# Mixture-of-experts layer of a vision block: down products with the weights stationary, summed in PSUM over all experts, gates applied to the activations

## What is computed

```
up_s   = einsum('th,seh->tse', xt, shared_up)                 # 2 shared experts
shared = einsum('tse,she->th', gelu(up_s), shared_down)
probs  = softmax(xt @ router_w.T)                             # 16 routed experts
gate   = top-4 of probs per token, elsewhere 0
act    = gelu(einsum('th,reh->tre', xt, routed_up)) * gate[:, :, None]
routed = einsum('tre,rhe->th', act, routed_down)
h      = h + shared + routed
```

## Time and profile before

| | us |
|---|---|
| three runs | 155.59, 155.68, 156.61 (median 155.68) |
| the profiled execution, whole | 155.6 |
| its span, first to last instruction | 153.8 |
| TensorE busy in the span | 148.0 (96%) |
| VectorE, ScalarE, GpSimd busy | 114.1, 102.2, 60.3 |
| granted TensorE clock | 1.00 |

### The profile page before, as it was taken

The page is one execution under the profiler, slowest core; times in us unless marked ns, Lnnn a source line. Parts: engine busy times, 40 slices in busy tenths (PEclk is TensorE's granted clock), DMA queues, the critical chain, the costliest instruction groups (busy, mean ns, idle before and its releaser), DMA issues.

```text
span 153.8 us, 3280 instructions
## 1 busy us (share of the span) xinstructions
PE 148.0 (96%) x1089; PEld 138.7 (90%) x1089; DVE 114.1 (74%) x370; ACT 102.2 (66%) x290; POOL 60.3 (39%) x50
## 2 busy tenths in 40 slices
PE   6989999999999999999999999999999999999992
PEld 2878799998897898999889999999999999999991
DVE  0058768768897776586765758997989679959982
ACT  0306999786689999999586398847583744636700
POOL 0004999456736544403119400332517323354000
PEclk9999999999999999999999999999999999999999
DMA  4999910000000499600000000000000000000004
GB/s 146 341 382 365 402 35 0 0 0 9 0 0 0 142 428 419 242 2 6 0 0 4 0 0 0 0 6 0 2 0 4 0 2 0 0 4 0 4 2 158
DMA packets 5892, 11.95 MB, mean 78 GB/s; under 512 B 931, under 2 KB 3699, under 8 KB 5747
## 3 DMA queue, kind: packets, MB, share of 16 engines
q1 hardware_dynamic: 4434, 9.79, 17.2%
q10 hardware_dynamic: 1440, 1.95, 3.6%
HBM read 11.13 MB, written 0.61 MB: 76 GB/s over the span
## 4 chain that ended last, share of the span: by engine, by line
PE 77%; ACT 8%; DVE 6%; DMA 3%; ACTq 2%; issue 1%; POOL 1%; DVEq 0%
PE bank L1047 61%; PE bank L1164 5%; PE bank L1071 5%; DMA aux_sb<-aux_w 3%; ACT probs L505 3%; PE bank L1136 2%; PE bank L1188 1%; ACT swapped L494 1%; ACT swapped L493 1%; PE bank L1152 1%; PE bank L1091 1%; DVE qk L726 1%; ACTq L241 1%; ACTq L244 1%; POOL swapped L399 1%
## 5 line engine op out<-in xcount | busy, mean ns | idle before, releaser
L414 POOL TENSOR_TENSOR exp_lo<-ffn_sb,exp_hi 128x512 fp32r<-128x512 f32 x18 | 23.5, 1314 | 40.5 <-ACT exp_hi L527 40.5
L839 DVE SCALAR_TENSOR_TENSOR h<-bank,gate,h 128x256 f32<-128x256 f32 (+1 forms) x80 | 32.3, 473 | 1.1 <-PE bank L1047 0.9
L1047 PE MATMUL bank<-exp_hi,act_hi 128*128 128x256 f32 (+1 forms) x90 | 25.5, 284 | 0.1
L1047 PE MATMUL bank<-exp_lo,act_hi 128*128 128x256 f32 (+1 forms) x90 | 25.2, 280 | 0.0
L1047 PE MATMUL bank<-exp_hi,act_lo 128*128 128x256 f32 (+1 forms) x90 | 25.2, 280 | 0.0
L819 DVE TENSOR_TENSOR act_lo<-act,act_hi 128x256 fp32r<-128x256 f32 (+1 forms) x36 | 17.9, 522 | 5.8 <-ACT act_hi L539 5.6
L1047 PE MATMUL bank<-hnT_hi,exp_hi 128*128 128x256 f32 (+1 forms) x72 | 21.8, 303 | 0.0
L536 ACT ACTIVATE act<-bank 128x256 f32<-128x256 f32 (+1 forms) x36 | 15.3, 424 | 9.6 <-PE bank L1047 9.4
L1047 PE MATMUL bank<-hnT_hi,exp_lo 128*128 128x256 f32 (+1 forms) x72 | 21.5, 298 | 0.0
L1047 PE MATMUL bank<-hnT_lo,exp_hi 128*128 128x256 f32 (+1 forms) x72 | 21.4, 297 | 0.0
L399 POOL TENSOR_TENSOR swapped<-swapped,sin_sb 128x512 f32<-128x512 f32 (+1 forms) x12 | 17.3, 1449 | 9.9 <-ACT swapped L494 9.9
(11 more groups left out here) (92 smaller groups left out, 368.2 us busy)
## 6 DMA issues: line engine op xcount, KB each, us to landing
ffn_sb<-w_ffn SPq DMA_DIRECT2D x6, 768.0 KB, 7.9
wqkv_sb<-w_qkv SPq DMA_DIRECT2D x4, 512.0 KB, 9.1
wo_sb<-w_o SPq DMA_DIRECT2D x1, 1024.0 KB, 11.4
x_sb<-xT ACTq DMA_DIRECT2D x2, 384.0 KB, 6.5
out<-h SPq DMA_DIRECT2D x2, 256.0 KB, 2.2
x_sb<-xT ACTq DMA_DIRECT2D x3, 128.0 KB, 4.0
wp_sb<-wpT SPq DMA_DIRECT2D x3, 128.0 KB, 3.5
wp_sb<-wpT ACTq DMA_DIRECT2D x3, 128.0 KB, 4.3
```

Source lines behind the costliest of these rows:

```text
L414: nc.gpsimd.tensor_tensor(exp_lo[:, e % SPLIT_RING, :], ffn_sb[:, e, :], exp_hi[:, e % SPLIT_RING, :].bitcast(F32), ALU.subtract).then_inc ...
L839: last = nc.vector.scalar_tensor_tensor(h[r, i, :], y, gate[r, i, one], h[r, i, :], ALU.mult, ALU.add)
L1047: last = nc.tensor.matmul(ps, a, b, start=(n == 0 and m == 0), stop=(n == len(pairs) - 1 and m == 2 and not more))
```

## The change

- **Down products** take the down weights as stationary operand (two halves of 128 output columns) and stream the activations of a span (256 or 336 columns), three matmuls for each half: 6 per unit. The result is transposed, 256 output columns on partitions, and stays in PSUM: four banks (4 to 7) sum all 18 experts.
- **Gates**: since tokens now lie along the free dimension, the gate of an expert must be there on all 128 partitions. `turn_gates` transposes `gate` on TensorE, `keep_gates` copies it to SBUF, SyncE stores it to a buffer in HBM (`gate_rows`) and, once that has landed, loads it back five times as a broadcast to 128 partitions (1, 1, 2, 6 and 6 experts; 4.85 MB in all, 303 KB for one expert).
- `gated(d)` (DVE) multiplies the gelu by the gate, in place in SBUF. `gelu` runs once for each unit; `act_high` (ACT) then rounds the gated values. The 80 scaled additions of `add_expert` go.
- **The end**: `keep_y0` (ACT) and `keep_y1` (DVE) copy the sums from PSUM, `turn_back(i)` transposes them (two transposes for each of 5 tiles), `add_experts(i)` adds them to `h` (5 additions), then the stores.
- The shared experts come first, before the gates are needed. The up products have only two PSUM banks for the first 12 units and four afterwards. Rings: 6 experts of weights, 12 units of `act`, 6 of `act_hi` and `act_lo`.
- The instruction lists of all engines are written anew, those of the attention stage too (other places for `wo_low`, `sine(11)`, `scores`, `attend`, `project_out`, `norm_apply` and others; the same calls).

```
+GATE_LOADS = [(0, 1), (1, 2), (2, 4), (4, 10), (10, NROUTED)]
 (SyncE)
-            for n, (a, z) in enumerate(OUT_STORES):
-                sp.wait_ge(y_added, ND - NP + n + 1)
+            sp.wait_ge(g_kept, 2)
+            sp.dma_start(gate_rows, gateT[:]).then_inc(s_gates, 16)
+            sp.wait_ge(s_gates, 16)
+            for n, (a, z) in enumerate(GATE_LOADS):
+                sp.dma_start(gates[:, a:z, :], gate_rows[a:z, :].unsqueeze(0).broadcast_to([P, z - a, T])).then_inc(l_gates[n], 16)
+            for a, z in OUT_STORES:
+                sp.wait_ge(out_made, z)
 (ScalarE)
-                nc.scalar.activation(act_hi[:, r, 0:n], bank[up_bank(u)][:, 0:n], ACT.Gelu).then_inc(act_hi_made, 1)
+            def act_high(d):
+                if d < UNGATED:
+                    act_e.wait_ge(act_made, unit_of(d) + 1)
+                else:
+                    act_e.wait_ge(act_gated, d - UNGATED + 1)
+                if d >= PART_RING:
+                    act_e.wait_ge(y_made, d - PART_RING + 1)
+                nc.scalar.activation(parts(act_hi, d), up_act(d), ACT.Copy).then_inc(act_hi_made, 1)
+            def keep_y0(b):
+                act_e.wait_ge(y_made, last_down(b))
+                nc.scalar.activation(yT[:, 0, span(b)], y_bank(b, 0), ACT.Copy).then_inc(y0_kept, 1)
 (VectorE)
+            def gated(d):
+                e, b = DOWNS[d]
+                dve.wait_ge(act_made, unit_of(d) + 1)
...
+                nc.vector.tensor_tensor(up_act(d), up_act(d), gates[:, e - NSHARED, span(b)], ALU.mult).then_inc(act_gated, 1)
+            def add_experts(i):
+                dve.wait_ge(y_turned, i + 1)
+                r = slice(0, TN[i])
+                nc.vector.tensor_tensor(h[r, i, :], bank[i % 4][r, 0:HID], h[r, i, :], ALU.add).then_inc(out_made, 1)
 (TensorE)
-                for k, i in enumerate(PIECES[p]):
-                    a = slice(i * P - SPANS[b][0], i * P - SPANS[b][0] + TN[i])
-                    last = three(y_bank(d)[0:TN[i], k * HID:(k + 1) * HID],
-                                 [(act_hi[:, act_slot(x, b), a], act_lo[:, act_slot(x, b), a],
-                                   exp_hi[:, x % SPLIT_RING, KH * P:], exp_lo[:, x % SPLIT_RING, KH * P:]) for x in both])
+                for m in range(KH):
+                    ws = slice(KH * P + m * P, KH * P + (m + 1) * P)
+                    for n, (j, a) in enumerate(((0, act_hi), (0, act_lo), (1, act_hi))):
+                        last = nc.tensor.matmul(y_bank(b, m), exp_part(e, j)[:, ws], parts(a, d),
+                                                start=(e == 0 and n == 0), stop=(e == NEXP - 1 and n == 2))
+            def turn_gates():
+                pe.wait_ge(r_gate, 1)
+                for i in range(TILES):
+                    turned, at = (bank[3], i * P) if i * P < CHUNK else (bank[2], 0)
+                    nc.tensor.transpose(turned[0:NROUTED, at:at + TN[i]], gate[0:TN[i], i, :],
+                                        ident[0:TN[i], 0:TN[i]]).then_inc(g_turned, 1)
+            def turn_back(i):
+                b = 1 if i * P >= SPANS[0][1] else 0
+                pe.wait_ge(y0_kept, b + 1)
+                pe.wait_ge(y1_kept, b + 1)
...
+                for m in range(KH):
+                    last = nc.tensor.transpose(bank[i % 4][0:TN[i], m * P:(m + 1) * P], yT[:, m, tile(i)], ident[:])
```

More of the change, by code:

```diff
@@ L420, in _ @@
                 qkv_low(n)
-            for n in range(0, 12):
+            for n in range(0, 11):
                 sine(n)
@@ L652, in _ @@
[L652 to L661 removed]
+            gelu(3)
+            act_high(0)
+            act_high(1)
+            router_exp()
+            gelu(4)
+            act_high(2)
+            gelu(5)
+            gelu(6)
+            act_high(3)
@@ new lines, in _ @@
+            high_parts(5)
+            gelu(7)
+            high_parts(6)
+            gelu(8)
+            gelu(9)
+            high_parts(7)
+            for n in range(10, 13):
+                gelu(n)
+            for n in range(4, 9):
+                act_high(n)
+            gelu(13)
+            act_high(9)
+            act_high(10)
+            gelu(14)
+            high_parts(8)
+            high_parts(9)
+            gelu(15)
+            for n in range(11, 14):
+                act_high(n)
@@ L672, in _ @@
+            act_high(27)
+            act_high(28)
+            gelu(34)
+            for n in range(29, 35):
+                act_high(n)
+            gelu(35)
+            act_high(35)
+            keep_y0(0)
+            keep_y0(1)
         @block.vector
@@ L1038, in _ @@
-            add_expert(17, 1)
-            add_expert(17, 2)
+            keep_gates()
+            act_low(2)
+            act_low(3)
+            gated(4)
+            gated(5)
+            act_low(4)
+            for n in range(6, 9):
+                gated(n)
+            for n in range(5, 8):
+                act_low(n)
+            for n in range(9, 12):
+                gated(n)
+            for n in range(8, 11):
+                act_low(n)
+            gated(12)
+            gated(13)
@@ new lines, in _ @@
+            act_low(11)
+            act_low(12)
+            gated(14)
+            act_low(13)
+            for n in range(15, 19):
+                gated(n)
+            for n in range(14, 18):
+                act_low(n)
+            for n in range(19, 23):
+                gated(n)
+            for n in range(18, 23):
+                act_low(n)
+            for n in range(23, 26):
+                gated(n)
+            act_low(23)
+            act_low(24)
+            gated(26)
+            gated(27)
@@ L1040, in _ @@
+            act_low(25)
+            act_low(26)
+            for n in range(28, 34):
+                gated(n)
+            for n in range(27, 34):
+                act_low(n)
+            gated(34)
+            gated(35)
+            act_low(34)
+            act_low(35)
+            keep_y1(0)
+            keep_y1(1)
+            for n in range(0, 5):
+                add_experts(n)
         @block.tensor
```

552 lines of the change are left out of this document (238 added, 314 removed).

## The result

| | median us | lowest to highest | runs |
|---|---|---|---|
| before | 156.18 | 155.59 to 156.98 | 22 |
| after | 155.60 | 154.94 to 156.53 | 22 |

The ratio of after to before is 0.9967, 95% interval 0.9954 to 0.998: the change saves 0.2 to 0.5%, some 0.5 us. The forecast was 156.8 us against 155.68, a ratio of 1.0072. The time lies in the wide range (154.2 to 159.3), just under the forecast's own one (155.7 to 157.9), and on the other side of no change.

What follows compares the result with a forecast made beforehand. TensorE, busy 148.0 of 153.8 us, was taken as the bound. Terms -2.5 + 0.5 + 1.1 + 0 + 0.4 + 1.9 - 0.3 = +1.1 on 155.6 gave 156.7, with 0.1 for the median 156.8; 8-in-10 range 154.2 to 159.3.

Steps and rivals of the forecast that it cites:

- part 3: About the router: four new TensorE waits, 1.3 us, less some 0.2 lost by the kernel before; net +1.1, bounds 0 and 2.
- part 5: Expert stage: VectorE, ScalarE and GpSimd fit on average, but VectorE and GpSimd exclude each other; +0.4 us, bounds 0 and 3.
- part 7: New lists before the experts: same work in other places closes some TensorE waits; -0.3 us, bounds +0.5 and -1.7.
- Rival D: Downs gain nothing, if streaming freshly written activations does not keep the distance by columns: 159.3 us, 5% chance.
- (a): At turn_norm(9): norm_apply(8) stands behind norm_stats(9) on VectorE, so hn of tile 4 comes later; TensorE waits 0.5 us.
- (b): At up(4): with only two banks it waits for gelu(2), late behind ScalarE's Gelu table load and copies; 0.2 us.
- (c): At down(0): TensorE waits for act_high(0) and act_low(0); 0.3 us.
- (d): At turn_gates: the chain from pick_top to the gate ends at 96.1, TensorE stands there from 95.77; 0.35 us.
- Part 4: Gates' way through HBM: hidden, 0; first load lands at 102.4, second 0.84 later, 2.4 us in hand before act_high(4).
- rival B: Gates land late; once the cover goes, each us of delay costs a us: 159 to 161 us, 10% chance.
- Rival A: VectorE and GpSimd shut each other out, delaying downs after the gates land and the last ten: 159 us, 22% chance.
- rival C: The lists pay: no router stall, VectorE never late, waits before the experts closed: 153.8 us, 18% chance.

Runs made afterwards that it cites:

- four_banks: The changed kernel with up(2) and up(3) writing PSUM banks 6 and 7 and up(5) before down(0): 154.71 us, ratio 0.992; run again 155.0, 0.993.
- one_extra: The changed kernel with the gates stored to HBM twice, so their loads begin one round trip later: 157.12 us, ratio 1.0062 to the kernel before.
- late_gates: The changed kernel with the gates stored to HBM three times, each store waiting for the one before: 160.51 us over four executions; the three unprofiled ones 159.99, ratio 1.0254.
- no_gating: The changed kernel without VectorE's 32 multiplications by the gate, the gates still sent through HBM: 155.55 us, ratio 0.9958 to the kernel before.
- two_products: The changed kernel without the third product of each down (low weights by high activations), 72 matmuls: 149.91 us, ratio 0.9615 to the kernel before.
- two_ungated: The changed kernel without the third product of each down and without the 32 gate multiplications: 147.32 us, ratio 0.9448 to the kernel before.
- late_paced: As late_gates, but the three large gate loads are issued only once the first two have landed: 161.44 us, ratio 1.0343 to the kernel before.

## Why the prediction was wrong

Most of the mechanisms were there. The sum failed at three terms: the new stalls (part 3) and the contention (part 5) were put too high, the gain of the new lists (part 7) too low, and all three errors lie on the same side.

- **Part 1, right.** The 269 distances after a down matmul of before, less the gaps in them, sum to 31.64 us (0.1176 each); after, 108 of 256 columns take 12.72 (0.1178) and 107 of 336 columns 16.41 (0.1533). That is -2.5, as forecast. Rival D fell.
- **Part 2, right.** +0.47 for the five transposes, forecast 0.5.
- **Part 3, failed: +0.48 measured, +1.1 forecast.** The gaps over the normal distances in the expert stretch are 1.05 us before and 1.53 after. Of the four waits, (a) came as 0.31 instead of 0.5; (b), the wait for a bank, came as 0.3 but two ups earlier, at `up(2)`; (c) came as 0.17 instead of 0.3; (d) did not come. Together 0.8 instead of 1.3. The larger slip is the deduction: "the kernel before loses some 0.2 here" was 1.05. I had read it from busy times, where a matmul's modelled end covers the gap in front of the next; the distances of starts show it. `four_banks` shows that 0.42 of what is left were waits for banks and for the order of two calls.
- **Part 4, right in the sum, wrong in the margin.** Hidden, 0: yes. "2.4 us in hand" was nothing: `one_extra` lost 1.5 us to a store of 1.65. That the first load was used at 102.77, near the 102.4 said, is luck: the store was issued 0.7 earlier and took 1.65 us instead of 2.2, and the load took 3.9 instead of 2.4. The step that failed is the second load: "0.84 later" was 2.0 later, 104.78. It is that one which `gated(5)`, and behind it `act_low(4)`, waits for. The price of rival B, a microsecond for each, held in `one_extra`; in the profiled execution of `late_gates` it was too low by the clock's 2.3.
- **Part 5, failed: 0 measured, +0.4 forecast.** `no_gating` bounds it at 0.14. Rows of 1.2 us beside GpSimd are there, as said; no down waited for them. Rival A, to which I gave 22%, did not come. With a sixth less work on TensorE the multiplications do cost time (2.7 us, `two_products` and `two_ungated`), by the exclusion or by their place in the chain. The rule of the Trainium skill (SBUF — State Buffer, "Who interferes with whom"), that a VectorE instruction with two SBUF inputs and a GpSimd instruction that reads SBUF exclude each other, agrees with the rows; what was wrong was taking its cost as a cost in time.
- **Part 6, right: +1.78 measured, +1.9 forecast.** The copy took 0.51, the five additions 1.74, the last ended 2.52 after the last matmul's start. Both of the forecast's terms hold to 0.1.
- **Part 7, failed: -0.9 measured (-1.0 by the cuts), -0.3 forecast.** It lay between my bounds. I argued that ScalarE, busy for 29.16 of 32.00 us, would be late next. It was as busy after, and TensorE still gained: the gaps came from the order of the lists, not from how much ScalarE had to do. This is the main part of rival C, which had 18%; its other half (no stall at all at the router) did not come, and neither did its 153.8.

Over the parts the errors are -0.6 (3), -0.4 (5), -0.6 to -0.7 (7) and -0.1 (6): -1.7 to -1.8, against a miss of 1.6. The measured parts sum to -0.6, so 0.9967 needs nothing else, within the 0.1 that the distances of starts leave open. What stays open is which call of the new lists closes which gap; I moved the whole lists and not single calls.

## What to carry to other kernels

Before pricing the stalls that a new order adds, measure those of the old order by distances of starts against the normal distance of the same shapes: here they were worth more (1.05 us in the expert stage and 2.6 in the attention stage, against a net 0.5 of new ones). When a rewrite changes two things, run each alone: here the part that gives the change its name paid nothing by itself. A side engine's contention is priced by what waits for it, not by how long its instructions get: 32 multiplications cost 0.14 us while TensorE needed 3.25 us for an expert, and 2.7 when it needed 2.7. Of a transfer issued as a small piece ahead of large ones, take the landing of the last piece that is needed, with the large ones already on the way.

## What the runs showed of the hardware

- Small loads issued just ahead of large ones landed late: two of 296 KB took 3.9 and 5.6 us in after, 3.3 and 4.1 with nothing behind them (`late_paced`). The store of 256 KB that I had priced them by took 2.2.
- In the 4.6 us in which TensorE stood still in `late_gates` the granted clock fell to its lower level, 2.8 us after the last matmul, and stayed there for 6.8 us; the 5.2 us of work in it cost 2.3 us on top of the wait. In `late_paced` two standstills (1.8 and 2.4 us) were enough in every execution; it fell 1.2 us after the second and lasted 3.4 us. After the 2.0 us of `one_extra` nothing was added: its expert stretch is 1.94 us longer than that of after.
- VectorE reading two operands from SBUF took 0.43 us alone and 1.24 beside a pass of GpSimd (after); the additions of the kernel before that read one operand from PSUM took 0.47 us beside such passes and alone.
- At the start of the kernel the full clock came between 4.15 and 7.29 us from one execution to the next, for the same instructions, and the wait for the first loads of `x` was between 0 and 0.9 us. Together with the wait for `aux_parts` they move the begin of tile 2 by up to 0.9 us, more than this change does. Comparing stretches between events behind it takes this out.
